# A GRU recurrence in which the reset gate's product also runs on split half-precision parts, and gates and state are handled in halves

## What is computed

```python
xz, xr, xh = x @ W_z, x @ W_r, x @ W            # for all 512 steps
vz, vr, vh = cond @ C_z + b_z, cond @ C_r + b_r, cond @ C + b
def step(h, xs):
    xzt, xrt, xht = xs
    z = sigmoid(xzt + h @ U_z + vz)
    r = sigmoid(xrt + h @ U_r + vr)
    hh = tanh(xht + r * h @ U + vh)              # (r * h) @ U
    h_new = (1.0 - z) * h + z * hh
    return h_new, h_new
out = x + all h_new, h0 = 0
```

## Time and profile before

| | us |
|---|---|
| median of 3 runs (lowest, highest) | 2313.96 (2313.88, 2314.53) |
| the profiled execution | 2313.02 |
| its span, first to last instruction | 2311.1 |

### The profile page before, as it was taken

How to read it: one execution, slowest core, us unless ns; L and a number is a source line. 1 busy time by engine, 2 the same in 40 slices (tenths; PEclk the granted TensorE clock), 3 DMA queues, 4 the chain that set the end, 5 groups by cost and what they waited for, 6 DMA issues and landing times.

```text
span 2311.1 us, 185969 instructions
## 1 busy us (share of the span) xinstructions
PE 2260.8 (98%) x82966; PEld 1885.7 (82%) x82966; DVE 1743.3 (75%) x7717; ACT 1036.7 (45%) x3091; POOL 686.8 (30%) x1546
## 2 busy tenths in 40 slices
PE   3999999999999999999999999999999999999998
PEld 2888888888888888888888888888888888888887
DVE  5777777777777777777777777777777777777776
ACT  3444444444444444444444444444444444444443
POOL 0333333333333333333333333333333333333332
PEclk9999999999999999999999999999999999999999
DMA  9110110110110110101101101101101011011001
GB/s 192 33 37 22 33 37 19 37 37 19 37 37 19 37 34 21 37 23 33 37 19 37 37 18 37 37 19 37 34 22 37 24 32 37 19 37 37 19 19 22
DMA packets 145367, 78.25 MB, mean 34 GB/s; under 512 B 9024, under 2 KB 140608, under 8 KB 145216
## 3 DMA queue, kind: packets, MB, share of 16 engines
q1 hardware_dynamic: 145216, 76.84, 13.8%
HBM read 43.25 MB, written 33.55 MB: 33 GB/s over the span
## 4 chain that ended last, share of the span: by engine, by line
PE 96%; SPq 2%; issue 1%; DMA 1%; ACT 0%; DVE 0%; ACTq 0%; POOLq 0%; POOL 0%; DVEq 0%
PE p_bank L238 43%; PE banks L230 39%; PE banks L260 15%; SPq L136 1%; DMA u<-in_L_cond_U_dram 1%; SPq L131 0%; PE p_bank L246 0%; SPq L146 0%; SPq L139 0%; ACT h_hi L366 0%; ACT table L398 0%; ACTq L397 0%; ACT L398 0%; ACT gate_c L373 0%; POOLq L48 0%
## 5 line engine op out<-in xcount | busy, mean ns | idle before, releaser
L238 PE MATMUL p_bank<-w_hi,x_t 128*32 128x384 f16 x16384 | 1189.1, 327 | 3.6 <-DVE w_lo L465 3.5
L238 PE MATMUL p_bank<-w_lo,x_t 128*32 128x384 f16 x8192 | 712.1, 327 | 0.0
L238 PEld LDWEIGHTS p_bank<-w_hi,x_t 128*32 128x32 f16 x16384 | 482.6, 97 | 144.4 <-issue 4.0
L230 PE MATMUL banks<-u,h_t 128*32 128x128 f32 x16352 | 544.9, 274 | 5.8 <-DMA u<-in_L_cond_U_dram 4.1
L230 PE MATMUL banks<-u,reset_t 128*32 128x128 f32 x16352 | 541.6, 273 | 1.4 <-issue 0.9
L230 PEld LDWEIGHTS banks<-u,h_t 128*32 128x32 f32 x16352 | 411.4, 109 | 107.7 <-DVE h_t L555 93.6
L200 POOL TENSOR_TENSOR kept<-keep,state 128x128 f32<-128x128 f32 x512 | 234.4, 458 | 887.3 <-ACT keep L370 887.3
L230 PEld LDWEIGHTS banks<-u,reset_t 128*32 128x32 f32 x16352 | 428.5, 109 | 82.8 <-DVE reset_t L535 66.5
L443 DVE SCALAR_TENSOR_TENSOR banks<-p_bank,x_down,base 128x128 f32<-128x128 f32 x1536 | 478.4, 342 | 4.2 <-issue 3.8
L212 POOL TENSOR_TENSOR result<-x_nat,state 128x128 f32<-128x128 f32 x512 | 234.2, 457 | 723.0 <-DVE state L553 723.0
L533 DVE TENSOR_TENSOR reset<-gate_r,state 128x64 f32<-128x64 f32 x1024 | 209.3, 204 | 210.6 <-ACT gate_r L368 210.5
(11 more groups left out here) (55 smaller groups left out, 1869.8 us busy)
## 6 DMA issues: line engine op xcount, KB each, us to landing
x_nat<-in_x_dram SPq DMA_DIRECT2D x256, 128.0 KB, 3.0
out_dram<-result SPq DMA_DIRECT2D x256, 128.0 KB, 2.7
w_stage<-in_L_cond_W_r_dram SPq DMA_DIRECT2D x4, 256.0 KB, 5.6
w_stage<-in_L_cond_W_z_dram SPq DMA_DIRECT2D x4, 256.0 KB, 8.4
w_stage<-in_L_cond_W_dram SPq DMA_DIRECT2D x4, 256.0 KB, 10.8
u<-in_L_cond_U_z_dram SPq DMA_DIRECT2D x4, 256.0 KB, 13.6
c_w<-in_L_cond_C_r_dram SPq DMA_DIRECT2D x4, 256.0 KB, 12.3
c_w<-in_L_cond_C_z_dram SPq DMA_DIRECT2D x4, 256.0 KB, 15.2
```

Of the source, the lines that this page charges most:

```text
L230: last = nc.tensor.matmul(out[part(j)], turned[:, part(q)], weights[:, q, cols(j)], start=first and q == 0, stop=q == Q - 1, skip_group_ch ...
L238: last = nc.tensor.matmul(p_bank[k][part(j), 0:G * N], x_t[:, c, part(q), a], w[b][:, :, q, cols(j)], start=f == 0, stop=f == GROUPS - 1, ...
```

## The change

Named in its parts, with the lines below cut to them:

1. `U_r` is split as `U_z` is (`ur`, a fifth entry of `SPLITS`), and its product is three half-precision products (`reset_product`): 48 matmuls, in the order h_hi first half x ur_hi, x ur_lo, h_hi second half x ur_hi, x ur_lo, h_lo first half x ur_hi, h_lo second half x ur_hi. Each half is waited for.
2. `h_hi` and `h_lo` are made in halves of 64 columns; `h_lo` now stands ahead of the R seed on VectorE.
3. The R sigmoid is in halves and has a per-partition `scale` operand (`r_down`); the tanh is in halves; r x h waits for its half.
4. `taken`, the new state and its transpose are in halves, in the order take 0, renew 0, take 1, turn 0, renew 1, turn 1.
5. Ahead of the loop: `U_r` is loaded ahead of the biases and the C matrices; the wait for `U` moves to step 1's C product; a sigmoid into `table` stands ahead of the loop on ScalarE, whose loop now begins at step 4; base, seeds and clearing matmuls are reordered.

```diff
-    UZ = G
-    SPLITS = (R, Z, C, UZ)
+    UZ, UR = G, G + 1
+    SPLITS = (R, Z, C, UZ, UR)
...
+        ur = [sb(n, [P, Q, E], f16) for n in ("ur_hi", "ur_lo")]
...
+        r_up, r_down = sb("r_up", [P, 1]), sb("r_down", [P, 1])
...
             load_weights(u[:, Z], U_z, s_u_in[Z])
+            load_weights(u[:, R], U_r, s_u_in[R])
             for g, b in enumerate((b_r, b_z, b_h)):
                 for p in range(J):
                     sp.dma_start(bias[part(p), g], b[cols(p)].unsqueeze(0).to_broadcast([B, N])).then_inc(s_bias_in, 16)
             for g, c in enumerate((C_r, C_z, C_h)):
                 load_weights(c_w[:, g], c, s_c_in[g])
             load_x(1, 1)
-            load_weights(u[:, R], U_r, s_u_in[R])
...
+            def reset_product(out, halves):
+                passes = [(h, a, b) for a in range(2) for h in range(HALVES) for b in range(2 - a)]
+                for n, (h, a, b) in enumerate(passes):
+                    if b == 0:
+                        pe.wait_ge((h_hi_ready, h_lo_ready)[a], halves[h])
+                    for q in range(Q // HALVES * h, Q // HALVES * (h + 1)):
+                        for j in range(J):
+                            last = nc.tensor.matmul(out[part(j)], (h_hi, h_lo)[a][:, part(q)], ur[b][:, q, cols(j)],
+                                                    start=False, stop=n == len(passes) - 1 and q == Q - 1,
+                                                    skip_group_check=True)
+                return last
+
+            def update_product(out):
                 for a, b in PARTS:
-                    if a == 1:
-                        pe.wait_ge(h_lo_ready, now)
                     for q in range(Q):
                         for j in range(J):
                             last = nc.tensor.matmul(out[part(j)], (h_hi, h_lo)[a][:, part(q)], uz[b][:, q, cols(j)],
...
-            pe.wait_ge(s_w_hi, G + 1)
-            pe.wait_ge(s_w_lo, G + 1)
-            for g in range(G):
-                pe.wait_ge(s_u_in[g], 16 * J)
-
-            def step(m, tt, last):
+            def step(m, tt, last, candidate_in=None):
...
-                product(cell(k, R), h_t, u[:, R], halves=[(h_t_ready, a) for a in halves]).then_inc(r_mm, 1)
-                update_product(cell(k, Z), now).then_inc(z_mm, 1)
+                reset_product(cell(k, R), halves).then_inc(r_mm, 1)
+                update_product(cell(k, Z)).then_inc(z_mm, 1)
...
+                if candidate_in is not None:
+                    pe.wait_ge(candidate_in, 16 * J)
                 product(cell(k, C), reset_t, u[:, C], halves=[(reset_t_ready, a) for a in halves]).then_inc(c_mm, 1)
...
+            step(0, 1, True, s_u_in[C])
             with pe.Fori(0, SETS - 3) as m:
-                for tt in range(1, SET + 1):
+                for tt in range(2, SET + 2):
                     step(m, tt, False)
-            for s in range(SET * (SETS - 3) + 1, T):
+            for s in range(SET * (SETS - 3) + 2, T):
...
+            nc.scalar.activation(table[:], w_up[:, 0:1], ACT.Sigmoid)
             act.wait_ge(x_in[1], 16 * J)
             act.wait_ge(x_summed, 2)
             sum_x(2, 0)
             act.wait_ge(s_z_scale, 1)
...
-                act.wait_ge(h_t_ready, HALVES * (s + 1) if last else act.snap(HALVES * s + HALVES))
-                nc.scalar.activation(h_hi[:], h_t[:], ACT.Copy, scale=2.0 ** POW).then_inc(h_hi_ready, 1)
+                now = s + 1 if first or last else act.snap(s + 1)
+
+                for a in range(HALVES):
+                    act.wait_ge(h_t_ready, HALVES * s + (a + 1) if first or last else act.snap(HALVES * s + (a + 1)))
+                    nc.scalar.activation(h_hi[:, half(a)], h_t[:, half(a)], ACT.Copy, scale=2.0 ** POW)\
+                        .then_inc(h_hi_ready, 1)
                 act.wait_ge(r_mm, now)
-                nc.scalar.activation(gate_r[:], cell(k, R), ACT.Sigmoid).then_inc(r_gate, 1)
+                for a in range(HALVES):
+                    nc.scalar.activation(gate_r[:, half(a)], half_cell(k, R, a), ACT.Sigmoid, scale=r_down[:]).then_inc(r_gate, 1)
                 act.wait_ge(z_mm, now)
                 nc.scalar.activation(keep[:], cell(k, Z), ACT.Sigmoid, scale=z_minus[:]).then_inc(z_keep, 1)
                 nc.scalar.activation(gate_z[:], cell(k, Z), ACT.Sigmoid, scale=z_down[:]).then_inc(z_gate, 1)
                 act.wait_ge(c_mm, now)
-                nc.scalar.activation(gate_c[:], cell(k, C), ACT.Tanh).then_inc(c_gate, 1)
+                for a in range(HALVES):
+                    nc.scalar.activation(gate_c[:, half(a)], half_cell(k, C, a), ACT.Tanh).then_inc(c_gate, 1)
...
+            for tt in range(SET):
+                step(0, tt, False, True)
             with nc.Fori(0, PASSES - 1, engines=[act.engine], hint_back_edge=True) as i:
                 nc.scalar.activation(table[:], z_minus[:], ACT.Sigmoid)
-                for tt in range(STEPS):
+                for tt in range(SET, STEPS + SET):
...
+                link(V.tensor_copy(r_down[:], w_down[:, UR:UR + 1]))
+                link(up_of(r_up[:], w_pow[:, UR:UR + 1], 2 * POW))
+                link(V.tensor_scalar(base[:, R], base[:, R], r_up[:], None, ALU.mult))
...
                 ahead = (tt + 1) % 2, (tt + 1) // SET % 2
+                for a in range(HALVES):
+                    dve.wait_ge(h_hi_ready, count(HALVES * s + (a + 1)))
+                    V.scalar_tensor_tensor(h_lo[:, half(a)], h_t[:, half(a)], 2.0 ** POW, h_hi[:, half(a)], ALU.mult,
+                                           ALU.subtract).then_inc(h_lo_ready, 1)
                 if not (last and tt == STEPS - 1):
                     if t == SET - 1:
                         dve.wait_ge(x_down_ready, count(now_m + 2))
                     dve.wait_ge(projected, count(s + 2))
                     seed(*ahead, (R,))
-                dve.wait_ge(h_hi_ready, now)
-                V.scalar_tensor_tensor(h_lo[:], h_t[:], 2.0 ** POW, h_hi[:], ALU.mult, ALU.subtract)\
-                    .then_inc(h_lo_ready, 1)
 
-                dve.wait_ge(r_gate, now)
                 for a in range(HALVES):
                     ready = count(HALVES * s + (a + 1))
+                    dve.wait_ge(r_gate, ready)
                     V.tensor_tensor(reset[:, half(a)], gate_r[:, half(a)], old[:, half(a)], ALU.mult).then_inc(reset_ready, 1)
                     dve.wait_ge(reset_ready, ready)
                     V.transpose(reset_t[:, half(a)], reset[:, half(a)]).then_inc(reset_t_ready, 1)
...
-                dve.wait_ge(c_gate, now)
-                V.tensor_tensor(taken[:], gate_c[:], gate_z[:], ALU.mult).then_inc(taken_ready, 1)
-                dve.wait_ge(taken_ready, now)
-                for a in range(HALVES):
-                    ready = count(HALVES * s + (a + 1))
+                ready = [count(HALVES * s + (a + 1)) for a in range(HALVES)]
+
+                def take(a):
+                    dve.wait_ge(c_gate, ready[a])
+                    V.tensor_tensor(taken[:, half(a)], gate_c[:, half(a)], gate_z[:, half(a)], ALU.mult).then_inc(taken_ready, 1)
+
+                def renew(a):
+                    dve.wait_ge(taken_ready, ready[a])
                     V.tensor_tensor(new[:, half(a)], taken[:, half(a)], kept[:, half(a)], ALU.add).then_inc(h_ready, 1)
-                    dve.wait_ge(h_ready, ready)
+
+                def turn(a):
+                    dve.wait_ge(h_ready, ready[a])
                     V.transpose(h_t[:, half(a)], new[:, half(a)]).then_inc(h_t_ready, 1)
+
+                take(0)
+                renew(0)
+                take(1)
+                turn(0)
+                renew(1)
+                turn(1)
```

More of the change, by code:

```diff
@@ L247, in total, with clear_bits @@
                 return last
+            def clear_bits(k):
+                for g in range(G):
+                    nc.tensor.matmul(banks[k][:, g], zeros[:, 0:P], zeros[:], start=True, stop=True).then_inc(s_bits, 1)
             def total_x(k, c, of, sets):
@@ L280, in _ @@
                 product(cell(1, g), cond_t, c_w[:, g], first=True).then_inc(s_base_mm, 1)
-            pe.wait_ge(s_zeros, 1)
             pe.wait_ge(s_base, G)
-            for k in range(2):
-                for g in range(G):
-                    nc.tensor.matmul(banks[k][:, g], zeros[:, 0:P], zeros[:], start=True, stop=True).then_inc(s_bits, 1)
+            clear_bits(1)
             pe.wait_ge(seeded, 1)
@@ L358, in _, with step @@
             act.wait_ge(s_z_scale, 1)
-            def step(i, tt, last):
+            def step(i, tt, last, first=False):
                 s = i * STEPS + tt
                 k = tt % 2
-                now = s + 1 if last else act.snap(s + 1)
-                act.wait_ge(h_t_ready, HALVES * (s + 1) if last else act.snap(HALVES * s + HALVES))
-                nc.scalar.activation(h_hi[:], h_t[:], ACT.Copy, scale=2.0 ** POW).then_inc(h_hi_ready, 1)
+                now = s + 1 if first or last else act.snap(s + 1)
```

(15 more changed lines are left out.)

34 lines of the change are left out of this document (22 added, 12 removed).

## The result

The changed kernel takes 2381.6 us (median of 4 runs, 2381.2 to 2382.4), the kernel before 2313.9 (2313.2 to 2314.5). The ratio is 1.0295, 95% interval 1.0282 to 1.0308: slower by 3%. Predicted were 2416 us, with 2365 to 2465 as the range. The profiled execution took 2381.24, so 68.2 us more than the 2313.0 of before, or 0.13 in each of the 511 steps where +0.20 was forecast.

The account below looks back on a forecast made before the run. The step was taken as bound equally by packed TensorE matmuls and the latency chain, 4.37 us each. +0.24 - 0.04 = +0.20 per step, times 511 = +102, outside 0: 2416 us, range 2365 to 2465.

Parts of the forecast that it names:

- The reading: Whole step: packed TensorE matmuls and the latency chain both fill 4.37 us, so shortening only one gains nothing.
- The first rival: R product: TensorE's packed work sets the pace, R falls 0.88 to 0.67, -107 us, 2207 us; chance 0.07.
- Part A: Tanh start to R load: the added `h_hi` copy lengthens it from 1.19 to 1.43 us, +0.24 per step.
- what `take(1)` costs in the path: VectorE between renew 0 and turn 0: transpose starts at 0.84 behind the tanh, 0.77 without take 1.
- The ScalarE slope: ScalarE activations: 0.90 ns per column, so 64 columns fewer save about 0.06 us.
- Rivals 2 and 3: ScalarE halves cheap: +0.02 per step, about 2327 us; or dear: +0.41, 2520, likelier 2465 to 2500. Chance 0.10 each.
- Part B: R load to tanh: 3.14 us instead of 3.18, -0.04 per step.
- the gap: Inside the R product: TensorE idles 0.17 us waiting for the second half of `h_hi`.
- Part C: Outside the steps: loop rounds 0 to +1 us, ahead of the loop about -1; counted as 0.
- The busy share: TensorE's busy time on the profile page: falls from 98% to about 90%.
- 18% free: TensorE: weight loading's 82% share, by the skill's rule, leaves 18% free, which speaks against TensorE setting the pace.

Follow-up runs that it names:

- Experiment 2: Changed kernel with the R product back in float32 from `h_t` and no scale operand in its sigmoid, halves kept: 2307.1 us, ratio 0.9978 to the kernel before.
- experiment 1: Changed kernel, R matmuls reading zeros and waiting for `h_t`, not the copy: 2329.1 us with Z waiting early for `h_lo`, 2234.7 us with that wait moved later.
- `imm_scale`: Changed kernel with the R sigmoid's per-partition scale operand replaced by a constant of the same value: 2381.5 us, ratio 1.0296 to the kernel before.
- experiment 5: Changed kernel with a projection group moved into R's gap (2375.3 us), with a constant scale in the R sigmoid (2381.5 us), with both (2328.0 and 2327.3 us).
- `gap_imm_2`: Changed kernel with a projection group in R's gap, a constant sigmoid scale, and the matmuls summing |x| ahead of the R product: 2327.3 us.
- `gap_fill`: Changed kernel with one projection group moved from ahead of C to between R's first and second half: 2375.3 us, ratio 1.0269 to the kernel before.
- the second kernel of experiment 1: Changed kernel with R matmuls reading zeros and waiting for `h_t`, and Z waiting for `h_lo` only ahead of its third pass: 2234.7 us, ratio 0.967.
- experiment 4: Changed kernel with tanh and `taken` whole again, the rest in halves: 2504.4 us with semaphore raises by two, 2437.3 us with raises by one.

## Why the prediction was right, and where it was off

**The reading** (both bounds in one place) holds. Experiment 2 cut the chain by 0.11 and gained 0.01; experiment 1 took the copy out, and the time fell until TensorE was packed. The first rival fell: TensorE's work per step did shrink (4.16 for 4.37 by its products), but R's first load waits for ScalarE in each step. Had it come to pass, its price was too high as well (77 us, not 107).

**Part A**, said +0.24, was +0.19. From the tanh's start:

| step | said | trace |
|---|---|---|
| take 0 | 0.25 | 0.26 |
| renew 0 | 0.51 | 0.52 |
| take 1 | 0.68 | 0.66 |
| turn 0 | 0.84 | 0.79 |
| `h_hi` | 1.12 | 1.07 |
| R load | 1.43 | 1.38 |

One term is mis-sized: what `take(1)` costs in the path. I took 0.17 between independent instructions, the distance from a transpose to the next addition. Here take 1 starts 0.14 behind renew 0, and turn 0 starts 0.13 behind take 1. Without take 1 the transpose would have followed renew 0 by 0.26; with it the distance is 0.27. The second `taken` fits into the latency of the first half and costs 0.01, where I charged 0.07. With the first `taken` 0.01 later than said, 0.05 is left: 0.05 x 511 = 26 us of the 34 by which the forecast was high. The ScalarE slope of 0.90 ns per column gave 0.25, 0.22 and 0.31 for the halves; the groups have 0.256, 0.221 and 0.311. Rivals 2 and 3 fall with these rows.

The Trainium skill (ScalarE: Activation LUTs, What ACT_TABLE_LOAD costs) gives 186 ns + 0.833 ns per column, 239 ns for a half; the trace has 256 for the copy and 221 for the tanh, so the formula holds within 18 ns. Its 93 ns for a per-partition operand agrees with 311 against 221: the sigmoid's halves in the kernel after, and in `imm_scale`, where the scale is a constant:
```profile
L389 ACT ACTIVATE gate_r<-banks 128x64 f32<-128x64 f32 x1024 | 173.0, 221 | 379.8 <-PE banks L269 379.8
```

**Part B**, said -0.04, was -0.06. R load to sigmoid 1.07 (said 1.07), the gap 0.15 (0.17), sigmoid to C load 0.90 (0.90), C matmul 2.00 behind the R load (2.02), C matmul to tanh 1.12 (1.12). The 0.02 is the smaller gap: the second half of `h_hi` is 0.38 behind the first. That packed work and chain meet at C as they do at R, with 0.05 between them in my sum, was right, and experiment 5 shows it: each edit alone gave 6 us or nothing, both gave 54.

**Part C**, said 0, is about 0. The round of the loop costs 0.37 a time, as said, but six times and not seven. Ahead of the loop it was 0.08 worse and not 1 better: x of steps 8 to 15 came at 50.49, as against 51.4 (47.12 + 4.25) by my estimate, but the first product hardly gained from it. The 0.08 says little: in `gap_imm_2` and `gap_fill`, whose part ahead of the loop is the same, the first product starts at 55.16 and 57.07, in one profiled execution each.

**The busy share** was forecast wrong. I said that it falls to about 90%; it stayed at 98%, although TensorE's loads wait 0.37 + 0.15 in each step. By the products (R 0.67, Z 0.67, projection 0.49, C 0.87, projection 1.46, in all 4.16) 0.34 of 4.50 is idle. The matmul ends in a trace are modelled and cover it: the last projection row ahead of R starts at 1211.66 and is drawn 0.34 long, up to R's start at 1211.99, while in packed stretches such rows follow each other by 0.16. The share of weight loads moved: 74% here, 82% before, 90% in the kernel of experiment 2. The Trainium skill (Trainium Kernel Development and Optimization, Performance Expectations), by which weight loading's share is the better measure, agrees with these three numbers. I had cited it and still made my forecast on the other row. But the share is no measure of what is left free: the second kernel of experiment 1, with no wait ahead of R, has 81% on its page, nearly the 82% of before. And the kernel before had no room on TensorE at its 82%, by the sum of its rows and by experiment 2. So the prediction's step from 82% to "18% free" was wrong, though the rival that it spoke against did fall.

So the loss came about as worked out. With the copy out of the path all that is left of the change gives 0.15 per step (experiment 1: 77 us against the kernel before), and the copy with its hand-over takes 0.29 of it back. The difference of the two is the measured loss by construction; what the experiment adds is how it divides. Whether tanh and `taken` in halves have a part in the 0.15 no run shows: with the copy out of the path the matmuls start 0.12 behind their load, about as much as these halves save. With the copy in the path they are worth 0.11 (experiment 4).

## What to carry to other kernels

Where packed work and a chain of latencies are equally long, ask of each edit which of the two it lengthens; a shorter product is worth nothing if its operand needs one more engine on the way and comes later than TensorE is free, as here. Edits that shorten only one bound are worth trying in pairs: 6 and 0 us alone were 54 together. And splitting small instructions in two pays when the second half fits into the latency of the first, and not because a half costs half.
